# A decoder layer on one core: query products 512 tokens wide, staged three units ahead

## Chip, cores and metric

The kernel runs on one core of a Trainium2 chip. The time is the device time of one execution in microseconds (us), median of the runs shown. Engines: TensorE (PE: matmuls and transposes; PEld is its weight load), VectorE (DVE), ScalarE (ACT), GpSimd (POOL), and SyncE (SP), which here only issues DMAs.

## What is computed

A decoder layer on x of 16 x 64 tokens, width 512, in float32. Cut to what matters:

```python
x = layernorm(x + self_attention(x))        # 32 heads of 16, 8 kv heads, rotary, causal
# second attention: H, KVH, D = 32, 8, 128
q = (x @ Wq).reshape(b, 64, 32, 128); k, v = (ctx @ Wk), (ctx @ Wv)   # 8 kv heads
q = q * cos + rotate_half(q) * sin          # k alike; cos, sin by position
a = softmax(where(mask == 0, -1e9, q @ k.T / sqrt(128)))
x = layernorm(x + (a @ v) @ Wo)
# feed-forward with a selection of rows and columns by clusters
dots = softmax(x @ centroids.T / 0.1); hits = dots > 0.01
y = where(any(hits, 1)[:, None] & any(hits, 0)[assignments][None, :], x @ weight.T + bias, 0)
out = layernorm(x + y)
```

## The kernel before

Everything stays in SBUF, tokens in 8 tiles of 128. Every float32 operand of a large product is split: `copy` on ACT (line 885) rounds it to the array's format ("high"), `low` on DVE (line 1379) or a subtraction on POOL makes the rest ("low"), and a product is three passes, high x high, high x low, low x high (`PASSES`).

The second attention runs as 32 units: a group g (0 to 7) is one kv head with its four query heads, and c (0 to 3) is a pair of token tiles, 256 tokens; unit u = 4 g + c. Each engine has its own program, and a function `slot(u, g, c)` in each writes out by hand what that engine does for the unit; slots 0 to 3 and the last are unrolled, the groups between run in a loop. The engines are held together by semaphores that count.

PE in a slot: `out_proj(u - 1, 1)` (12 matmuls of 512 columns, line 651, the second half of the last unit's output product), the query products of unit u + 2 for the first head pair (`q_pair`, line 424, 24 matmuls of 256), the key and value products of unit u + 1 (`kv_pair`, 24 of 256), `p_turn(u)` (four transposes of the probabilities, line 618), 12 matmuls of the second head pair, `pv(u)` (value products, line 635, 12 of 256), the other 12, `k_turn(u + 1)` (line 644), `out_proj(u, 0)`, and `scores(u + 1)` (lines 665 and 667). In slots 0 to 2 two context tiles are turned first (`ctx_turn`, line 608).

The softmax chain of a unit goes through all engines: `corrections` (ACT), `masked_max2` (DVE, lines 1596 to 1602), `shift` (POOL, line 1290), `exponents` (ACT, line 1049), `total2` (DVE, lines 1606 and 1608), `normalise` (POOL, line 1295), then `p_turn` on PE. Then `p2_high` and `p2_low` round the probabilities for `pv`, and `at2_high` and `at2_low` its result for `out_proj`.

Queries take this way: PE leaves them in banks 0 and 1; DVE multiplies them with the cosine and sine tables (`rope2_q`, lines 1538 and 1539, into `u1q` and `u2q`); POOL adds the halves (`sum_q`, lines 1262 and 1263); SP moves them between partitions with four DMAs (`stage_q`, line 354) into `q_st`; ACT and DVE round them (`q_high`, `q2_low`), with `q_high(u + 1)` ahead of `exponents(u)` in ACT's order from unit 3 on; `scores` uses them. Keys go `rope2_k`, `sum_k` (line 1267), `k_turn`, `k_high`, `k2_low`.

Weights of a group arrive in SBUF once a group: `load_kv` in c = 0, `load_q` (1024 KB into `w2q_raw`) in c = 1, `load_o` in c = 2 into the same place. The query weights of the next group are rounded at the end of the slot with c = 1, two of the four low parts by POOL (`wq_low`, line 1271) and two by DVE; key and value weights in c = 2 (POOL, line 1277), output weights in c = 0 (`wo_low`, POOL line 1282 and DVE).

The tail: units 30 and 31 have no query products any more. The slots of these units are written out apart and hold feed-forward work besides: `fw_turn` (line 764, transposes of its weights), `x3_turn` (line 770, of the normalised tiles), `cluster_dots` (777, 779), `dots_turn` (788), `dense(t)` (795 and 800, twelve matmuls and one for the bias), and after them the counts (869, 872), from which DVE gets the row mask (line 1844) and then does `choose` (1851) and the statistics of each tile.

## Time and profile before

| | us |
|---|---|
| median of 3 runs | 824.31 (824.14 to 825.51) |
| profiled execution | 824.27, span 822.5 |
| PE busy | 765.3 |
| DVE busy | 623.6 |
| POOL busy | 391.8 |
| ACT busy | 319.4 |

The span is the time from the first to the last instruction of the one execution that the profiler took; the rest of its 824.27 us lies around it. Busy time of an engine leaves out waits, branches and the issuing of DMAs. Two things are not in the table and have to be read from the trace: at which places the busiest engine is not busy, and what ended its wait there.

### The profile page before, as it was taken

The numbers are of one execution on the slowest core, as the hardware profiler recorded it, in microseconds if no ns is written. First come the engines' busy times: TensorE is split into PE (matmuls) and PEld (weight loads), VectorE is DVE, ScalarE is ACT, GpSimd is POOL, SyncE is SP. The second block draws the span as 40 slices with busy tenths as digits, with TensorE's granted clock in tenths as the row PEclk, the third lists the DMA queues.
The fourth block names the chain that finished last, engine by engine and source line by source line (L and its number), as shares of the span: only waits on it lengthen the run. The fifth ranks groups of instructions, "written<-read, shape, count | busy, mean of one in ns | idle before, by whom it ended". The sixth has DMA issues, their size and how long they took to land.

```text
span 822.5 us, 15514 instructions
## 1 busy us (share of the span) xinstructions
PE 765.3 (93%) x5520; PEld 691.1 (84%) x5520; DVE 623.6 (76%) x1179; ACT 319.4 (39%) x669; POOL 391.8 (48%) x415
## 2 busy tenths in 40 slices
PE   3689999989899999999999999999999999998894
PEld 2677777779899998999999899999989999997773
DVE  4678888877887777678677767767776777788767
ACT  4455555562443323333332333333232333324313
POOL 7566666664544354444445444544444454443102
PEclk9899999999999999999999999999999999999998
DMA  9500004012333222123322212322221322131002
GB/s 256 124 18 17 16 16 118 3 55 52 85 104 96 52 78 78 27 58 84 87 51 77 77 26 66 84 79 51 77 77 26 75 82 73 45 84 27 1 1 103
DMA packets 104048, 53.50 MB, mean 65 GB/s; under 512 B 80208, under 2 KB 89552, under 8 KB 104016
## 3 DMA queue, kind: packets, MB, share of 16 engines
q1 hardware_dynamic: 103184, 51.51, 24.0%
q10 hardware_dynamic: 576, 1.05, 0.4%
q0 software_dynamic: 256, 0.52, 0.2%
q8 instruction: 19, 0.31, 0.2%
q14 instruction: 13, 0.11, 0.0%
HBM read 32.62 MB, written 2.10 MB: 42 GB/s over the span
## 4 chain that ended last, share of the span: by engine, by line
PE 70%; DVE 15%; issue 8%; POOL 3%; ACT 2%; DMA 1%; SPq 1%; DVEq 0%; ACTq 0%; POOLq 0%
PE bank L424 30%; PE bank L651 18%; PE s_bank L665 4%; DVE arena_r L1379 4%; PE bank L474 2%; PE s_bank L667 2%; PE bank L635 2%; PE bank L498 2%; DVE small L1467 2%; DVE arena_f L1461 1%; PE s_bank L635 1%; POOL arena_f L1295 1%; PE s_bank L498 1%; DMA arena_f<-in_L_attn_Wo 1%; PE bank L618 1%
## 5 line engine op out<-in xcount | busy, mean ns | idle before, releaser
L424 PE MATMUL bank<-arena_r 128*128 128x256 f32 (+1 forms) x2496 | 334.6, 290 | 2.8 <-DVE arena_r L1379 2.0
L424 PEld LDWEIGHTS bank<-arena_r 128*128 128x128 f32 x2496 | 313.3, 191 | 14.3 <-issue 2.4
L885 ACT ACTIVATE arena_r<-bank 128x256 fp32r<-128x256 f32 (+2 forms) x250 | 105.4, 459 | 227.7 <-PE bank L618 98.1
L651 PE MATMUL bank<-arena_r 128*128 128x512 f32 x768 | 191.5, 398 | 0.0
L651 PEld LDWEIGHTS bank<-arena_r 128*128 128x128 f32 x768 | 139.7, 189 | 27.3 <-DVE arena_r L1379 0.6
L1379 DVE TENSOR_TENSOR arena_r<-bank,arena_r 128x256 fp32r<-128x256 f32 (+2 forms) x218 | 100.3, 487 | 57.8 <-ACT arena_r L885 57.6
L885 ACT ACTIVATE arena_r<-arena_f 128x512 fp32r<-128x512 f32 (+2 forms) x178 | 103.8, 637 | 85.6 <-DMA arena_f<-arena_f 71.5
L1379 DVE TENSOR_TENSOR arena_r<-arena_f,arena_r 128x512 fp32r<-128x512 f32 (+1 forms) x114 | 115.9, 1030 | 19.1 <-ACT arena_r L885 19.0
L1262 POOL TENSOR_TENSOR arena_f<-arena_f 128x256 f32<-128x256 f32 x64 | 54.2, 846 | 91.6 <-DVE arena_f L1539 91.5
L1290 POOL TENSOR_TENSOR arena_f<-arena_f,small 128x512 f32<-128x512 f32 x32 | 33.4, 1044 | 109.9 <-DVE small L1602 109.9
L1295 POOL TENSOR_TENSOR arena_f<-arena_f,small 128x512 f32<-128x512 f32 x32 | 44.0, 1375 | 64.7 <-DVE small L1608 64.7
L1565 DVE TENSOR_TENSOR arena_f<-bank,arena_f 128x512 f32<-128x512 f32 x64 | 43.9, 686 | 24.2 <-PE bank L651 24.2
L885 ACT ACTIVATE arena_f<-s_bank 128x512 f32<-128x512 f32 (+1 forms) x35 | 20.5, 586 | 100.2 <-PE s_bank L667 92.6
L667 PE MATMUL s_bank<-arena_r 128*128 128x64 f32 x256 | 57.9, 244 | 0.0
L665 PE MATMUL s_bank<-arena_r 128*128 128x128 f32 x256 | 57.3, 295 | 0.0
L885 ACT ACTIVATE arena_r<-s_bank 128x512 fp32r<-128x512 f32 (+1 forms) x99 | 52.2, 528 | 1.1 <-PE s_bank L498 0.7
L1263 POOL TENSOR_TENSOR arena_f<-arena_f 128x256 f32<-128x256 f32 x64 | 50.1, 783 | 0.0
L667 PEld LDWEIGHTS s_bank<-arena_r 128*128 128x128 f32 x256 | 49.0, 191 | 1.2
L665 PEld LDWEIGHTS s_bank<-arena_r 128*128 128x128 f32 x256 | 49.0, 191 | 1.2
L1216 POOL TENSOR_TENSOR arena_f<-arena_f,small 128x512 f32<-128x512 f32 x32 | 34.3, 1072 | 32.8 <-DVE small L1463 32.8
L1596 DVE TENSOR_TENSOR arena_f<-s_bank,arena_f 128x512 f32<-128x512 f32 x32 | 22.1, 691 | 36.5 <-ACT arena_f L885 36.5
L1379 DVE TENSOR_TENSOR arena_r<-s_bank,arena_r 128x512 fp32r<-128x512 f32 (+1 forms) x83 | 47.8, 576 | 1.1 <-ACT arena_r L885 0.9
(147 smaller groups left out, 1065.2 us busy)
## 6 DMA issues: line engine op xcount, KB each, us to landing
arena_f<-arena_f SPq DMA_DIRECT2D x128, 128.0 KB, 2.5
arena_f<-in_L_xattn_Wq SPq DMA_DIRECT2D x8, 1024.0 KB, 5.5
arena_f<-in_L_xattn_Wo SPq DMA_DIRECT2D x8, 1024.0 KB, 5.5
arena_f<-in_x SPq DMA_DIRECT2D x8, 256.0 KB, 2.9
arena_f<-in_x SPq DMA_DIRECT2D x1, 2048.0 KB, 15.4
arena_f<-in_L_xattn_Wk SPq DMA_DIRECT2D x8, 256.0 KB, 3.0
arena_f<-in_L_xattn_Wv SPq DMA_DIRECT2D x8, 256.0 KB, 3.3
arena_f<-in_ctx SPq DMA_DIRECT2D x8, 256.0 KB, 3.1
```

What stands on the lines that cost most here:

```text
L424: mm = pe.matmul(bank, lhs(a, c), rhs(b, c), start=(c == 0 and n == 0), stop=(c == chunks - 1 and n == 2))
L651: mm = pe.matmul(BO2[i][:], at2[a][:, h, i * P:(i + 1) * P], w2o_s[b][:, h, :], start=(h == 0 and n == 0), stop=(h == HG - 1 and n == 2))
L665: pe.matmul(BS2[h][:, at:at + 2 * S], high, kT2[:, :, b * S:(b + 1) * S], start=True, stop=False, skip_group_check=True)
L667: mm = pe.matmul(BS2[h][:, at + S:at + 2 * S], low_, kT2[:, 0, b * S:(b + 1) * S], start=False, stop=True, skip_group_check=True)
L885: act.activation(dst, src, ACT.Copy).then_inc(done, 1)
L1216: pool.tensor_tensor(cut(p1[u], b=8, k=S), cut(sc1[u % 2], b=8, k=S), bcast(mx1[u], 2, S), ALU.subtract).then_inc(s_sub, 1)
L1262: pool.tensor_tensor(u1q[:, 0, j, :], u1q[:, 0, j, :], u2q[:, 1, j, :], ALU.subtract).then_inc(c_qs, 1)
L1263: pool.tensor_tensor(u1q[:, 1, j, :], u1q[:, 1, j, :], u2q[:, 0, j, :], ALU.add).then_inc(c_qs, 1)
L1290: pool.tensor_tensor(cut(p2, b=8, k=S), cut(sc2, b=8, k=S), bcast(mx2, 2, S), ALU.subtract).then_inc(c_sub, 1)
L1295: pool.tensor_tensor(cut(p2, b=8, k=S), cut(p2, b=8, k=S), bcast(sm2, 2, S), ALU.mult).then_inc(c_pn, 1)
L1379: dve.tensor_tensor(dst, src, f32(high), ALU.subtract).then_inc(done, 1)
L1565: dve.tensor_tensor(y, banks[6 + i][:], y, ALU.add).then_inc(c_acc, 1)
```

## The change

Query products of units 2 to 31 are made 512 tokens wide: one head pair j for the two units of a token half cp, so that a *turn* k (2 to 31) serves two units with one head pair. A turn is run in slot u for k = u + 3 (turns 2 and 3 both in slot 0), and half of its second bank's products stand to either side of `pv`. Units 0 and 1 keep the narrow form. `rope2_q` works bank by bank on 512 columns, `sum_q` is two additions of 512 columns in place of four of 256, at one place of the slot; `stage_q` moves one head pair of two units in four DMAs to `q_high_st` or one of two `q_low_st`. Query weights are loaded and rounded by halves (`load_half`): heads 2 and 3 in c = 1, heads 0 and 1 in c = 3 of the group before, their low parts all on POOL. Late context tiles get buffers of their own. In the tail, the feed-forward weight turns and the first two `x3_turn` stand in unit 29, the 30th, `dense(0)` in unit 30, and the orders of `norm_tile`, `pick`, `x3_turn`, `dense` and of the banks are changed.

```diff
+        def turn_of(g, c):
+            j, ahead = (c + 1) % 2, c + 2 + c % 2
+            return j, (ahead % UN) // 2, g + ahead // UN
+        def staged(u, c):
+            return 128 * u + 128 if isinstance(u, int) and u < 2 else 64 * (u + 1 - c % 2) + 192
 # SyncE
-                sp.wait_ge(c_qs, 4 * u + 4)
+                sp.wait_ge(c_qs, 2 * k + 2)
+                if starts_with(u):
+                    sp.wait_ge(c_wkl, 2)
+                    load_half(1, 0)
+                    stage_q(2, 0, 1)
+                    sp.wait_ge(c_wol, 4)
...
+                elif c == 3 and is_group(g + 2):
+                    sp.wait_ge(c_wkl, 2 * g + 4)
+                    load_half(g + 2, 0)
+                if is_unit(u + 3):
+                    stage_q(u + 3, j, cp)
 # TensorE
+            def q_turn(k, j, cp, f, chunks=range(EC)):
+                if chunks[0] == 0:
+                    pe.wait_ge(c_rq, 2 * k + f - 1)
+                tok = slice(4 * cp * P, 4 * cp * P + 4 * P)
+                for e in chunks:
+                    for n, (a, b) in enumerate(PASSES):
+                        mm = pe.matmul(BQ2[f][:], w2q_s[a][:, e, j, f, :], xT[b][:, e, tok],
+                                       start=(e == 0 and n == 0), stop=(e == EC - 1 and n == 2))
+                if chunks[-1] == EC - 1:
+                    mm.then_inc(c_q, 1)
...
-                if not first:
+                if first:
+                    pe.wait_ge(s_x1l, T)
+                    q_turn(2, 0, 1, 0)
+                    q_turn(2, 0, 1, 1)
+                else:
                     out_proj(u - 1, 1)
-                if q_next:
-                    pe.wait_ge(c_wql, 4 * g2 + 4)
-                    q_pair(u + 2, c2, 0)
+                    if q_next:
+                        pe.wait_ge(c_wql, 4 * gq + 2 * j + 2)
+                        q_turn(u + 3, j, cp, 0)
                 if kv_next:
                     pe.wait_ge(c_wkl, 2 * g1 + 2)
                     kv_pair(u + 1, c1)
                 p_turn(u)
-                if q_next:
-                    pe.wait_ge(c_rq, 2 * u + 4)
-                    q_proj(c2, 1, 0)
+                if first:
+                    q_turn(3, 1, 1, 0)
+                elif q_next:
+                    q_turn(u + 3, j, cp, 1, range(0, 2))
                 pv(u, c, first)
-                if q_next:
-                    q_proj(c2, 1, 1).then_inc(c_q, 1)
+                if first:
+                    q_turn(3, 1, 1, 1)
+                elif q_next:
+                    q_turn(u + 3, j, cp, 1, range(2, 4))
 # GpSimd
+            def sum_q(k):
+                pool.wait_ge(c_rq, 2 * k + 2)
+                pool.tensor_tensor(u1q[:, 0], u1q[:, 0], u2q[:, 1], ALU.subtract).then_inc(c_qs, 1)
+                pool.tensor_tensor(u1q[:, 1], u1q[:, 1], u2q[:, 0], ALU.add).then_inc(c_qs, 1)
...
+                if c == 3 and is_group(g + 2):
+                    wq_low(g + 2, 0)
+                    wq_low(g + 2, 1)
 # VectorE
+            def rope2_q(k, cp, f):
+                dve.wait_ge(c_q, 2 * k + f + 1)
+                if f == 0:
+                    dve.wait_ge(d_qs, 64 * k + 128)
+                tok = slice(4 * cp * P, 4 * cp * P + 4 * P)
+                dve.tensor_tensor(u1q[:, f], banks[f][:], cosT[:, tok], ALU.mult)
+                dve.tensor_tensor(u2q[:, f], banks[f][:], sinT[:, tok], ALU.mult).then_inc(c_rq, 1)
...
-                if split and c == 1:
-                    wq_low(g + 1, 2)
-                    wq_low(g + 1, 3)
...
 # VectorE, unit 31
-            norm_tile(4)
             masked_max2(v, c)
+            norm_tile(4)
             accumulate(v - 1, c - 1, 1)
...
-            dve.tensor_tensor(pair_sum[:], ident[:, 0:NC], ident[:, NC:P], ALU.add).then_inc(f_ps, 1)
```

## Rows read from the trace of the kernel before

**Rows 1.** Page, part 1: busy us, share of the span, instructions

```profile
PE 765.3 (93%) x5520; PEld 691.1 (84%) x5520; DVE 623.6 (76%) x1179; ACT 319.4 (39%) x669; POOL 391.8 (48%) x415
```

**Rows 2.** Busy time by stage: length, then PE, PEld, DVE, ACT, POOL, clock

```profile
243.99:709.25 465.26, 462.19 (x3391) 427.42 (x3390) 341.51 (x625) 158.69 (x350) 216.01 (x223) 1.00 0.25 66
...
726.89:744.53 17.64, 17.64 (x132) 16.40 (x132) 13.51 (x30) 4.82 (x11) 6.99 (x9) 1.00 0.38 101
744.53:763.55 19.02, 16.51 (x120) 14.29 (x120) 16.45 (x37) 9.61 (x21) 3.83 (x5) 1.00 0.12 26
763.55:784.37 20.82, 18.25 (x92) 14.43 (x92) 16.02 (x35) 5.88 (x18) 3.77 (x5) 0.92 0.00 1
```

**Rows 3.** Timeline, a slot with c = 1: start, length, instructions, idle before

```profile
441.01 2.60 PEld L651 LDWEIGHTS bank<-arena_r 128*128 128x128 f32 x12
443.64 5.93 PEld L424 LDWEIGHTS bank<-arena_r 128*128 128x128 f32 x48
449.52 0.25 PEld L618 LDWEIGHTS bank<-ident,arena_f 128*128 128x128 f32 x2
...
454.22 0.69 DVE L1538 TENSOR_TENSOR arena_f<-bank,arena_f 128x512 f32<-128x512 f32 x1
```

**Rows 4.** Who waited for whom, whole span, PE: total, times, longest

```profile
PE bank L618 <- POOL arena_f L1295: 6.5, 8, 2.6
```

**Rows 5.** Timeline, the slot with c = 2 behind it

```profile
458.65 2.60 PEld L651 LDWEIGHTS bank<-arena_r 128*128 128x128 f32 x12
459.30 2.65 SPq L354 DMA_DIRECT2D arena_f<-arena_f  x4
463.80 1.15 ACT L885 ACTIVATE arena_r<-arena_f 128x512 fp32r<-128x512 f32 x2 [4.32 <-DMA arena_f<-arena_f]
467.94 0.20 PEld L618 LDWEIGHTS bank<-ident,arena_f 128*128 128x128 f32 x2 [0.73 <-POOL arena_f L1295]
477.07 2.60 PEld L651 LDWEIGHTS bank<-arena_r 128*128 128x128 f32 x12
```

**Rows 6.** POOL: two groups (busy, mean ns, idle before), two timeline rows

```profile
L1271 POOL TENSOR_TENSOR arena_r<-arena_f,arena_r 128x512 fp32r<-128x512 f32 x16 | 20.6, 1290 | 28.9 <-ACT arena_r L885 28.9
L1234 POOL TENSOR_TENSOR arena_f<-arena_f 128x512 f32<-128x512 f32 x8 | 10.2, 1280 | 1.2 <-DVE arena_f L1399 0.6
448.84 0.74 POOL L1262 TENSOR_TENSOR arena_f<-arena_f 128x256 f32<-128x256 f32 x1 [0.38 <-DVE arena_f L1539]
456.95 1.17 POOL L1262 TENSOR_TENSOR arena_f<-arena_f 128x256 f32<-128x256 f32 x1
```

**Rows 7.** Timeline, a slot with c = 0

```profile
494.72 2.60 PEld L651 LDWEIGHTS bank<-arena_r 128*128 128x128 f32 x12
505.01 0.41 DVE L1379 TENSOR_TENSOR arena_r<-s_bank,arena_r 128x256 fp32r<-128x256 f32 x1
505.29 0.42 PEld L635 LDWEIGHTS bank<-arena_r 64*128 64x128 f32 x6
507.84 0.20 PEld L644 LDWEIGHTS bank<-ident,arena_f 128*128 128x128 f32 x2 [0.15 <-issue]
```

**Rows 8.** Timeline, slot 0, which follows the first attention

```profile
207.45 0.69 DVE L1379 TENSOR_TENSOR arena_r<-bank,arena_r 128x512 fp32r<-128x512 f32 x1 [0.93 <-ACT arena_r L885]
211.70 3.11 PE L424 MATMUL bank<-arena_r 128*128 128x256 f32 x24 [1.17 <-DVE arena_r L1379]
218.22 0.62 PE L635 MATMUL bank<-arena_r 64*128 64x256 f32 x6 [1.42 <-DVE arena_r L1379]
```

**Rows 9.** Timeline, unit 31 and the end

```profile
767.46 0.69 DVE L1596 TENSOR_TENSOR arena_f<-s_bank,arena_f 128x512 f32<-128x512 f32 x1
773.92 0.44 PE L618 MATMUL bank<-ident,arena_f 128*128 128x128 f32 x2 [2.57 <-POOL arena_f L1295]
778.63 5.89 PE L651 MATMUL bank<-arena_r 128*128 128x512 f32 x24
799.97 0.69 DVE L1844 CAST mask_i<-bank 128x512 int32<-128x512 f32 x1 [1.93 <-PE bank L872]
```

More of the change, by code:

```diff
@@ L394, in _ @@
                 load_ctx(t)
-            stage_q(1)
+            stage_first(1)
             for u in range(UN):
                 slot(u, 0, u)
-            with sp.Fori(1, G2 - 1) as g:
+            with sp.Fori(1, G2 - 2) as g:
                 for c in range(UN):
                     slot(UN * g + c, g, c)
+            for c in range(UN):
+                slot(UN * (G2 - 2) + c, G2 - 2, c)
             sp.wait_ge(c_wkl, 2 * G2)
@@ L754, in _ @@
                 slot(u, 0, u)
-            with pe.Fori(1, G2 - 1) as g:
+            with pe.Fori(1, G2 - 2) as g:
                 for c in range(UN):
                     slot(UN * g + c, g, c)
-            for u in range(U - UN, U - 2):
-                slot(u, G2 - 1, u % UN)
+            for c in range(UN):
+                slot(UN * (G2 - 2) + c, G2 - 2, c)
+            slot(U - UN, G2 - 1, 0)
             def fw_turn(c):
@@ L811, in _ @@
             fw_turn(1)
+            p_turn(v)
+            pe.wait_ge(f_wl, 1)
+            fw_turn(2)
+            pv(v, v % UN, False)
+            k_turn(v + 1, False)
+            pe.wait_ge(f_wl, 2)
+            fw_turn(3)
+            pe.wait_ge(f_wl, 3)
+            x3_turn(0)
+            out_proj(v, 0)
+            pe.wait_ge(f_wl, 4)
+            x3_turn(1)
+            scores(v + 1, False)
+            v = U - 2
+            out_proj(v - 1, 1)
+            kv_pair(v + 1, UN - 1)
             pe.wait_ge(d_fc, 16)
@@ L816, in _ @@
             mm.then_inc(f_cT, 1)
+            pe.wait_ge(f_xl, 2)
+            dense(0, range(0, 3))
             p_turn(v)
-            pe.wait_ge(f_wl, 1)
-            fw_turn(2)
-            pe.wait_ge(f_wl, 2)
-            fw_turn(3)
+            dense(0, range(3, EC))
             pe.wait_ge(f_cl, 1)
@@ L1079, in slot @@
                     act.wait_ge(c_q, 2 * u + 6)
-                    for h in range(HG):
-                        wq_high(g + 1, h)
+                    wq_high(g + 1, 2)
+                    wq_high(g + 1, 3)
                 if split and c == 2:
@@ L1115, in _ @@
                 slot(u, 0, u)
-            with act.Fori(1, G2 - 1) as g:
+            with act.Fori(1, G2 - 2) as g:
                 for c in range(UN):
                     slot(UN * g + c, g, c)
-            for u in range(U - UN, U - 2):
-                slot(u, G2 - 1, u % UN)
+            for c in range(UN):
+                slot(UN * (G2 - 2) + c, G2 - 2, c)
+            slot(U - UN, G2 - 1, 0)
             def fw_high(c):
@@ L1354, in root @@
                 pool.tensor_tensor(rstd8[:, t:t + 1], var8[:, t:t + 1], half8[:, 0:1], ALU.pow).then_inc(f_pow, 1)
-            for u in range(U - UN, U - 2):
-                slot(u, G2 - 1, u % UN)
+            slot(U - UN, G2 - 1, 0)
             root(0, 0)
+            shift(U - 3)
             root(1, 1)
+            normalise(U - 3)
+            sum_k(U - 2)
+            root(2, 2)
             shift(U - 2)
-            root(2, 2)
             root(3, 3)
@@ L1723, in _ @@
                 slot(u, 0, u)
-            with dve.Fori(1, G2 - 1) as g:
+            with dve.Fori(1, G2 - 2) as g:
                 for c in range(UN):
                     slot(UN * g + c, g, c)
-            for u in range(U - UN, U - 2):
-                slot(u, G2 - 1, u % UN)
+            for c in range(UN):
+                slot(UN * (G2 - 2) + c, G2 - 2, c)
+            slot(U - UN, G2 - 1, 0)
             def norm_tile(t):
@@ L1763, in pick @@
             def pick(t):
+                dve.wait_ge(f_sel, 1 + sum(t >= b for _, b in GROUPS))
                 dve.wait_ge(f_dense, t + 1)
```

345 lines of the change are left out of this document (210 added, 135 removed).

## The prediction

> **What bounds the kernel now.** I read the busy line first, then busy time and clock by stage, then who waited for whom, then one stretch of the main loop in order of time. TensorE (PE) is the busiest engine, with 93% of the span [rows 1]. Split by stage, the 32 units of cross attention are the body: from 243.99 to 709.25 us PE is busy 462.2 of 465.3 us at its full clock (1.00 granted, 2.4 GHz), and the loose stretches are the last two units, from 744.53 us on [rows 2], and the place where the loop is entered [rows 8]. So in the loop a microsecond of matmul time taken away is a microsecond of span, unless the softmax chain beside it becomes later than PE. I call a *slot* the work from one `out_proj(u - 1, 1)` to the next, c its place among the four of a group. The slot with c = 1 takes 17.64 us (first load of weights at 441.01, the next slot's at 458.65) [rows 3, 5], the one with c = 2 takes 18.42 (458.65 to 477.07) [rows 5], and c = 3 17.65 (to 494.72) [rows 7]. With c = 2 PE waits for `normalise`; the waits list eight such idles, 6.5 us [rows 4], of which unit 31 has 2.57 [rows 9] and unit 30 0.9, so six of about 0.5 in the loop.
>
> **Why c = 2 is late.** The staged queries of the next unit are issued by SyncE (SP) at 459.30, ScalarE can round them at 463.80 (4.50 us later), and its exponentials stand behind them; `normalise` and then `p_turn`, the four transposes, come at 467.94, 4.14 us after the landing and 9.29 into the slot [rows 5]. In c = 1 `p_turn` starts 8.51 us into it (441.01 to 449.52), led by PE's own queue [rows 3].
>
> **1. Wide products.** Before, a unit's queries are 48 matmuls of 256 columns; after, 24 of 512, for 30 turns (units 0 and 1 keep the old form). Starts of weight loads give the spacing: 12 of 512 columns take 2.63 us (441.01 to 443.64), 219 ns each; the 48 of 256 take 5.88 (443.64 to 449.52), 122.5 each [rows 3]. 48 x 122.5 - 24 x 219 = 0.62 us a turn; I take 0.60, since a switch of width costs a little. Bounds: 0.5 to 0.65. In slots 1 to 28 that is 28 x 0.60 = 16.8 us; the turns of units 2 and 3 are both in slot 0.
> The rows put a matmul of 256 columns 13 ns above half of one of 512 (122.5 against 109.5). The Trainium skill, TensorE: Matmul & The Clock Gate, Back-to-back issue gap, gives N/2.4 + 2.5 ns for one matmul after another, so two of 256 would cost only some 3 ns more than one of 512: an estimated 0.08 us a turn, 2 us in all. This trace disagrees with it at 256 columns, and the row decides; what that outcome would be here is rival C.
>
> **2. Staging.** A turn k now serves a head pair of two units, three slots ahead. Its sums on GpSimd (POOL), before four of 256 a unit in two pairs (0.74 us where DVE is away), are two of 512 at the end of the slot; the nearest row is the first attention's sum of two 512-wide arrays, 1280 ns [rows 6]. The four DMAs carry the same 128 KB each. In odd slots (c = 1, 3) the queries of the next unit come from the turn just made, in even slots from one a slot older. So the late landing of c = 2 goes: -6 x 0.78 (18.42 - 17.64) = -4.7 us. The odd slots get a new date. The slot's last ropes start at 454.22, 13.2 into it, led by the end of the query products [rows 3], so at 12.6 after; two of about 0.64 give 13.9, two sums of 1.28 less their overlap 16.4, the issue 16.46; the slot is 17.04 long, so SP issues 0.58 before its end, the queries land 3.92 into the odd slot, and `p_turn` can go at 8.1. PE arrives at 2.63 + 2.63 + 24 x 0.1225 = 8.2. Forecast: no idle, with 0.1 us to spare. If sums run 0.3 us longer each, it is 14 x 0.5 = 7 us.
>
> **3. Slots with c = 0.** VectorE (DVE) there also does one `wo_low` ahead of `p2_low`; the second `p2_low` runs from 505.01 for 0.41 us, 10.7 after the slot's start at 494.72 (the first ends at 10.3), and PE starts the value products at 505.29, 10.57 [rows 7]. After, PE could be there at 9.95 and the DVE date doesn't move (it isn't led by PE): 0.4 idle. 7 x 0.4 = +2.8 us; bounds 0 to 0.6 each. `sum_k` no longer stands behind a query sum, which frees the 0.17 us that the k turns of c = 0 wait (0.15 idle at 507.84) [rows 7]: about -0.8 in all.
>
> **4. Rounding of weights.** DVE loses two `wq_low`, POOL makes all four, two at the end of c = 1 and two of c = 3, each 1290 ns [rows 6]. In c = 1 they end 16.4 + 2.55 = 19.0, 1.95 into c = 2, where PE asks for them at 2.63 after `out_proj`: hidden with 0.7 spare. The shift of the softmax needs POOL at 3.3 into a slot: hidden too. The halves of the weights are loaded nearly a slot ahead of their rounding: nothing.
>
> **5. The front.** Before, slot 0 idles 1.17 us ahead of the key products and 1.42 ahead of the value products [rows 8]. After, it first waits for `x1_low` of the last tile (207.45 + 0.69, against a start at 207.41): +0.8. Then 48 wide matmuls, 10.5 us, in place of 48 narrow, 5.9. They cover the first idle; the value products wait again about 0.6 for DVE, which has two more ropes ahead of `p2_low`. I get the end of slot 0 at 228.05 against 225.46: +2.6. In slot 1 `q_turn(4)` asks for weights of group 1 at 231.5. The chain: rope of turn 3 waits for the staging of turn 2 to land (issue about 220.2, plus 4.5), ropes to 227.6, sums to 230.15, two roundings to 232.7: 1.2 idle, less the 0.6 of its narrow products: +0.6. Bounds for the two together: +1 to +6.
>
> **6. The tail.** Slots 29 to 31 now have no query products; feed-forward turns and one `dense` more stand in them. Slot 29 was 17.64 full of PE work [rows 2]. After: 5.6 us of `out_proj` and keys, 1.0 of `fw_turn`, then `p_turn` at about 8.75 (landing 3.93, plus 4.14, plus statistics and a `norm_tile` on DVE ahead of `total2`); 2.1 idle; then value products 2.2 later, `out_proj(u, 0)` 2.1 behind them (DVE's `at2_low`), scores to 17.95: +0.3. Slot 30 was 19.02; by the same chain it is 18.15, with `dense(0)` inside: -0.9. In slot 31 the mask step no longer waits behind `norm_tile(4)`: it starts about 1.8 in place of 3.9 us into the slot (767.46), `p_turn` comes at 8.7 in place of 10.37 (773.92), `pair_sum` is gone from DVE's part of the chain, and `x3_turn(4)` no longer stands before the value products: the last `out_proj` ends at 18.5 in place of 20.8 (778.63 + 5.89 by its rows, 784.37 by the start of its successor): -2.3 [rows 2, 9]. Behind it runs the chain statistics, `x3_turn(7)`, cluster dots, hits, the two matmuls of counts; 799.97 is the date of the row mask, and from then on DVE is busy without a gap to the end [rows 9]. `pick(1)` costs 0.45 on it; half a `dense` fewer ahead of the second matmul and `pick(3)` out of it give back 1.35: -0.9. Since DVE sets the end, the `dense` moved forward gains nothing there.
>
> **The sum**, against the profiled execution (span 822.5, time 824.27; the median of the runs is 824.31): front +2.6 + 0.6; slots 2 to 28: 27 x 0.60 = -16.2 (the 28th is in the +0.6 of slot 1), -4.7, -0.8, +2.8; tail +0.3 - 0.9 - 2.3 - 0.9. Together -19.5: span 803.0, time 804.8.
>
> **Rivals.** *A, as above*: 801 to 809. *B, staged queries land late in odd slots.* For it: only 0.1 us of slack, and POOL's 256-wide sums already stretch from 0.74 to 1.17 us (456.95) while DVE works on the weights [rows 6]. Against: at that point DVE works on PSUM. Late by 0.5 to 0.8 in 14 slots it costs 7 to 11 us: 812 to 816. *C, no gain by width*: a wide query product takes twice a narrow one. Then 30 x 0.60 = 18 us are lost, of which the idles that PE no longer has in c = 0 give back 2.8: 820, a gain of half a per cent. Against: the output products have the same widths and operands and take 219. *D, slower.* One mechanism: POOL's two sums are stretched throughout as that one is (1.6 times, 4.1 us in place of 2.5). Landing is 1.6 late, 1.5 idle in 14 odd slots (+21), and weights come at 3.6 in place of 1.95 in c = 2, +1 in 7 slots: 805 + 28 = 833. It turns to a loss once the sums take more than about 3.6 us (19.5 gained against 14 + 7 slots). Beside it stands the Trainium skill, GPSIMD Engine Reference, Key points: it shares its SBUF interfaces with VectorE and contends with instructions of two SBUF inputs. The trace agrees with it in the 1.17 us; that DVE reads PSUM where the new sums stand is the reason for the small chance.
>
> **Chances.** A 0.68, B 0.21, C 0.04, D 0.04, and 0.03 for better than A (tail chains shorter than I count). The range 800.5 to 813.5 takes in A and the better half of B. A measurement of this kernel can tell about 0.2%, 1.6 us. Faster 0.92, same 0.03, slower 0.05.
>
> **What would show it.** In the profile after: 512-column matmuls at 219 ns in the query lines; slots of 17.05 with c = 1, 2, 3 and about 17.45 with c = 0; no idle of PE behind `normalise` in c = 2. B shows as ScalarE waiting for the DMA beyond 4.1 us in odd slots and PE behind `normalise`; D as sums of 2 us. I am wrong by the front if slot 1 starts after 230, and by the tail if slot 31 starts less than 15 us earlier than now (763.55).

## The result, and the profile after

The changed kernel takes 817.78 us (median of 4 runs, 817.54 to 818.55) beside 824.47 us for the kernel before in the same comparison: ratio 0.9921 (95% interval 0.9906 to 0.9935). That is a gain of 6.7 us where I had forecast 19.5, so the time lies outside the range of 800.5 to 813.5, on its slow side. The profiled execution has a span of 816.0 us, against 822.5.

The busy line of the page, which answers to [rows 1]: TensorE is still at 93%; it has 720 instructions less, and only 6.7 us less of busy time.

```profile
PE 758.6 (93%) x4800; PEld 649.0 (80%) x4800; DVE 607.5 (74%) x1165; ACT 317.6 (39%) x669; POOL 392.2 (48%) x369
```

Busy time by stage answers to [rows 2] (length, PE, PEld, DVE, ACT, POOL, granted clock, DMA share, GB/s). The stretches are the slots 2 to 28, slot 29, slot 30, slot 31 up to the last output product's end, and the rest.

```profile
247.51:721.42 473.91, 472.12 (x2872) 405.38 (x2871) 340.62 (x638) 163.24 (x365) 223.83 (x190) 1.00 0.27 69
721.42:741.10 19.68, 16.59 (x108) 14.62 (x108) 16.12 (x35) 8.31 (x17) 4.85 (x5) 0.91 0.15 35
741.10:759.84 18.74, 17.14 (x109) 14.07 (x109) 14.42 (x31) 6.62 (x15) 4.86 (x5) 1.00 0.00 1
759.84:778.07 18.23, 16.94 (x91) 13.51 (x91) 15.40 (x33) 5.79 (x18) 3.61 (x4) 1.00 0.00 1
778.07:816.00 37.93, 24.18 (x115) 18.36 (x113) 26.48 (x69) 9.55 (x20) 5.47 (x10) 0.90 0.15 56
```

From the starts of the slots (first load of weights) the 6.5 us of the two profiled spans split as follows:

| part | before | after | difference | forecast |
|---|---|---|---|---|
| start of slot 0 | 206.51 | 205.38 | -1.1 | 0 (no part of the change) |
| slots 0 to 2 | 55.96 | 60.35 | +4.4 | +2.6 |
| slots 3 to 28 | 464.39 | 455.69 | -8.7 | -18.3 |
| slot 29 | 17.65 | 19.68 | +2.0 | +0.3 |
| slot 30 | 19.02 | 18.74 | -0.3 | -0.9 |
| slot 31 to the end | 58.97 | 56.16 | -2.8 | -3.2 |

The -1.1 us ahead of slot 0 are no gain of the change: the other two profiled executions of the changed kernel reach slot 0 some 1.3 and 2.3 us later than this one, with a mean granted clock of 0.87 and 0.79 in their first 40 us for 0.91 here (0.87 before).

Ten of the 13 us that are missing are in the loop. There the slots with c = 1, 2 and 3 take 17.40 to 17.46 us (but for unit 5's, 19.03), where before had 17.64 to 17.67 (18.33 to 18.44 with c = 2), and those with c = 0 17.56 (17.80 to 17.83). So the late landing of c = 2 went as forecast; of what was to come from the width a third did. Of the eight waits for `normalise` [rows 4] three are left, one in the loop and those of slots 29 and 31:

```profile
PE bank L690 <- POOL arena_f L1420: 4.1, 3, 1.8
```

The timeline of TensorE shows where. First a slot of the kernel before that [rows 3] shows by its loads of weights, now by the matmuls themselves (start, length, instructions):

```profile
441.04 2.99 PE L651 MATMUL bank<-arena_r 128*128 128x512 f32 x12
443.87 5.92 PE L424 MATMUL bank<-arena_r 128*128 128x256 f32 x48
449.62 0.38 PE L618 MATMUL bank<-ident,arena_f 128*128 128x128 f32 x2
...
449.98 1.67 PE L424 MATMUL bank<-arena_r 128*128 128x256 f32 x12
451.57 0.62 PE L635 MATMUL bank<-arena_r 64*128 64x256 f32 x6
...
452.48 1.70 PE L424 MATMUL bank<-arena_r 128*128 128x256 f32 x12
454.02 0.38 PE L644 MATMUL bank<-ident,arena_f 128*128 128x128 f32 x2
```

Then the same slot after, and below it the loads of weights of its first three groups:

```profile
459.58 2.99 PE L723 MATMUL bank<-arena_r 128*128 128x512 f32 x12
462.41 2.88 PE L658 MATMUL bank<-arena_r 128*128 128x512 f32 x12
465.13 3.04 PE L484 MATMUL bank<-arena_r 128*128 128x256 f32 x24
468.00 0.38 PE L690 MATMUL bank<-ident,arena_f 128*128 128x128 f32 x2
...
468.35 1.64 PE L658 MATMUL bank<-arena_r 128*128 128x512 f32 x6
469.92 0.62 PE L707 MATMUL bank<-arena_r 64*128 64x256 f32 x6
...
470.82 1.68 PE L658 MATMUL bank<-arena_r 128*128 128x512 f32 x6
472.34 0.38 PE L716 MATMUL bank<-ident,arena_f 128*128 128x128 f32 x2
...
459.55 2.60 PEld L723 LDWEIGHTS bank<-arena_r 128*128 128x128 f32 x12
462.18 2.68 PEld L658 LDWEIGHTS bank<-arena_r 128*128 128x128 f32 x12
464.90 3.05 PEld L484 LDWEIGHTS bank<-arena_r 128*128 128x128 f32 x24
```

The reader is to take starts of matmuls, one group to the next: 12 of 512 columns take 465.13 - 462.41 = 2.72 us, 227 ns each, and 48 of 256 columns 449.62 - 443.87 = 5.75 us, 120 ns each. The unbroken half of a turn thus goes from 24 x 120 = 2.88 to 2.72, 0.16 us. The other half is cut into two short groups, which stand between transposes (`p_turn`, `k_turn`) and the value products with their 64 rows; I call this a change of tile form. These groups hardly move: 449.98 to 451.57 is 1.59 before and 468.35 to 469.92 is 1.57 after; 452.48 to 454.02 is 1.54 and 470.82 to 472.34 is 1.52. Together 0.20 us a slot, and that is what the slots show. The loads tell another story because they run ahead: the first load of a group stands 0.23 us before its matmul (462.18 against 462.41), but at the first group of a slot, which follows short matmuls, only 0.03 (459.55 against 459.58). The 2.63 us from which I took 219 ns began at such a first load and ended at one that was already ahead.

### The profile page after: what moved, and what is told of

It is laid out like the page before. It is cut to its first block, busy times and chain, and to the rows that moved or that the text cites. A ratio compares the mean times of both kernels' runs of the same rounds, so it can differ in the third digit from the quotient of the medians.

```text
span 816.0 us, 13861 instructions
## 1 busy us (share of the span) xinstructions
PE 758.6 (93%) x4800; PEld 649.0 (80%) x4800; DVE 607.5 (74%) x1165; ACT 317.6 (39%) x669; POOL 392.2 (48%) x369
## 4 chain that ended last, share of the span: by engine, by line
PE 64%; DVE 19%; issue 6%; POOL 4%; ACT 2%; DMA 2%; SPq 2%; DVEq 0%; ACTq 0%; POOLq 0%
PE bank L723 17%; PE bank L658 17%; PE bank L484 10%; DVE arena_r L1512 5%; PE s_bank L737 3%; PE bank L534 2%; PE s_bank L739 2%; PE bank L707 2%; PE bank L558 2%; DVE small L1600 2%; DVE arena_f L1594 1%; PE s_bank L707 1%; ACT arena_r L979 1%; PE s_bank L558 1%; DMA arena_f<-in_L_attn_Wo 1%
## 5 line engine op out<-in xcount | busy, mean ns | idle before, releaser
L723 PE MATMUL bank<-arena_r 128*128 128x512 f32 x768 | 192.2, 399 | 0.9 <-DVE arena_r L1512 0.9
L658 PE MATMUL bank<-arena_r 128*128 128x512 f32 x720 | 185.2, 400 | 2.2 <-POOL arena_r L1396 1.6
L723 PEld LDWEIGHTS bank<-arena_r 128*128 128x128 f32 x768 | 139.9, 189 | 28.2 <-DVE arena_r L1512 1.3
L658 PEld LDWEIGHTS bank<-arena_r 128*128 128x128 f32 x720 | 130.7, 188 | 31.5 <-POOL arena_r L1396 2.1
L484 PE MATMUL bank<-arena_r 128*128 128x256 f32 (+1 forms) x1056 | 146.7, 295 | 1.5 <-DVE arena_r L1512 0.6
L484 PEld LDWEIGHTS bank<-arena_r 128*128 128x128 f32 x1056 | 137.4, 191 | 9.0 <-DVE arena_r L1512 1.5
L1512 DVE TENSOR_TENSOR arena_r<-arena_f,arena_r 128x512 fp32r<-128x512 f32 (+1 forms) x100 | 92.9, 937 | 17.6 <-ACT arena_r L979 17.5
L1387 POOL TENSOR_TENSOR arena_f<-arena_f 128x512 f32<-128x512 f32 x30 | 39.2, 1306 | 114.2 <-DVE arena_f L1681 114.2
L1420 POOL TENSOR_TENSOR arena_f<-arena_f,small 128x512 f32<-128x512 f32 x32 | 44.0, 1376 | 61.0 <-DVE small L1750 61.0
L1415 POOL TENSOR_TENSOR arena_f<-arena_f,small 128x512 f32<-128x512 f32 x32 | 34.1, 1065 | 64.9 <-DVE small L1744 64.9
```

Of the source, the lines that this page charges most:

```text
L484: mm = pe.matmul(bank, lhs(a, c), rhs(b, c), start=(c == 0 and n == 0), stop=(c == chunks - 1 and n == 2))
L658: mm = pe.matmul(BQ2[f][:], w2q_s[a][:, e, j, f, :], xT[b][:, e, tok], start=(e == 0 and n == 0), stop=(e == EC - 1 and n == 2))
L723: mm = pe.matmul(BO2[i][:], at2[a][:, h, i * P:(i + 1) * P], w2o_s[b][:, h, :], start=(h == 0 and n == 0), stop=(h == HG - 1 and n == 2))
L1387: pool.tensor_tensor(u1q[:, 0], u1q[:, 0], u2q[:, 1], ALU.subtract).then_inc(c_qs, 1)
L1415: pool.tensor_tensor(cut(p2, b=8, k=S), cut(sc2, b=8, k=S), bcast(mx2, 2, S), ALU.subtract).then_inc(c_sub, 1)
L1420: pool.tensor_tensor(cut(p2, b=8, k=S), cut(p2, b=8, k=S), bcast(sm2, 2, S), ALU.mult).then_inc(c_pn, 1)
```

## The experiments

**The width, undone.** `q_turn` with each product in two runs of 256 columns; all the rest is the changed kernel.

```diff
-                for e in chunks:
-                    for n, (a, b) in enumerate(PASSES):
-                        mm = pe.matmul(BQ2[f][:], w2q_s[a][:, e, j, f, :], xT[b][:, e, tok],
-                                       start=(e == 0 and n == 0), stop=(e == EC - 1 and n == 2))
+                for i in range(chunks[0] * P // width, (chunks[-1] + 1) * P // width):
+                    for e in range(EC):
+                        for n, (a, b) in enumerate(PASSES):
+                            mm = pe.matmul(BQ2[f][:, width * i:width * i + width], w2q_s[a][:, e, j, f, :],
+                                           xT[b][:, e, at + width * i:at + width * i + width],
+                                           start=(e == 0 and n == 0), stop=(e == EC - 1 and n == 2))
```

> The changed kernel with each query product over 512 tokens issued as two of 256 columns, the first half of the columns through all its 12 matmuls and then the second; staging, sums, ropes, POOL's order and the tail stay as changed. So the width is undone and all else is kept. Theory A (the width is worth what the starts of the matmuls give: 0.227 us for 512 columns and 0.120 for 256, 12 x (2 x 0.120 - 0.227) = 0.16 us in each of the two halves of a turn that runs unbroken, and about 0.02 us in each of the halves that end in a change of tile form): the ordinary slot goes from 17.44 to 17.64 us, 28 slots and the four turns of slot 0 add 6 us, about 824 us, as the kernel before. Theory B (my prediction: 0.60 us a slot, from the starts of the weight loads 0.219 and 0.1225): the slot goes to 18.05 us, +17, about 835 us. Theory C (the wait for the value products' low halves on VectorE sets the slot, so the width is idle): no change, 817 to 818 us.

Measured: 822.69 us, beside 817.90 for the changed kernel; its ordinary slots are 17.64 to 17.66 us. Theory A holds by the slots and my price of 0.60 us a slot falls. The medians differ by 4.8 us and not by 6, in part because the slots with c = 0 also take 17.64: the 0.13 us by which they were longer is hidden again. In the timeline both groups of 24 take 2.88 us:

```profile
465.13 3.04 PE L665 MATMUL bank<-arena_r 128*128 128x256 f32 x24
468.01 3.05 PE L484 MATMUL bank<-arena_r 128*128 128x256 f32 x24
470.89 0.38 PE L698 MATMUL bank<-ident,arena_f 128*128 128x128 f32 x2
```

**The repetition** that stood beside it:

> The changed kernel once more, beside the next three, so that each difference is taken on one chip. Expected: the ratio to the kernel before stays 0.992 (817.8 us beside 824.4). In the trace of its first execution the slots stood 17.43 to 17.46 us apart where before has 17.64 to 17.66, save one, unit 5's, with 19.03 us, in which TensorE waited 1.57 us for the normalised weights. Theory A (an accident of the transfers in the window of that execution): the 19.03 us slot is gone or elsewhere, and the others are 17.43 to 17.46 again. Theory B (the order of the queue in the loop's first pass): it comes back in the same slot with 18.9 to 19.1 us.

Measured: 817.90 us, ratio 0.9913 (0.989 to 0.9937). The ordinary slots are 17.40 to 17.46 again (slot 27 takes 17.69, behind a late landing), and unit 5's slot is the long one again: theory B by its place, though 19.40 us lies above its 18.9 to 19.1. More on it below.

**Only the cut half narrow.** The same edit for the second dimension half alone (`width = 2 * P if f == 1`).

> The changed kernel with only the second dimension half's product (the one cut in two parts, around the value products) issued in 256 columns; the first, unbroken one keeps 512. Theory A (at a change of tile form TensorE waits for the last matmul's end, 0.39 us after its start for 512 columns and 0.28 for 256, which takes back most of what six wide ones gain): +0.02 to 0.05 us in each of its two places, slots at 17.48 to 17.54 us, +1 to +3 us in all, 819 to 821 us. Theory B (the gain is by the columns, wherever they run): 2 x 0.08 us, slots at 17.60 us, +4.5 us, 822.3 us.

Measured: 818.61 us; slots of 17.50, +0.06. The two places take 1.60 and 1.55 us in place of 1.57 and 1.52. Theory A by the slots; the 0.7 us of the medians is within their spread. Six wide matmuls gain 0.03 us here where six in a long stream gain 0.08. (Unit 5's slot takes 17.50 here.)

```profile
468.38 1.67 PE L665 MATMUL bank<-arena_r 128*128 128x256 f32 x12
469.98 0.62 PE L715 MATMUL bank<-arena_r 64*128 64x256 f32 x6
...
470.88 1.70 PE L665 MATMUL bank<-arena_r 128*128 128x256 f32 x12
472.43 0.38 PE L724 MATMUL bank<-ident,arena_f 128*128 128x128 f32 x2
```

The mechanism of theory A, a wait at the end of the group, is not what the trace shows. Read one by one, the starts in the first of the two places lie 314, 231, 236, 228, 233 and 327 ns apart in the changed kernel, and 201, then ten of 116 to 121, then 209 in this one. The long interval ahead of the value products costs both widths nearly the same (100 and 89 ns more than in a stream), and so does the one behind the transposes (87 and 81). In the second place the last interval, ahead of transposes, is 232 and 123: no such wait at all. Most of the lost gain lies between: the wide ones stand 228 to 240 ns apart all through these short groups, the narrow ones 113 to 125. The first group of a slot, 12 wide ones behind short matmuls and with no change of form after them, starts alike (316, 237, 228, 232, 232) and only then reaches 227.

**Four runs of 128 columns**, the same edit with `width = P`:

> The changed kernel with each query product over 512 tokens issued as four of 128 columns, one after the other. It looks for the form of the cost of a matmul. Theory A (columns at 2.4 GHz and a fixed 13.5 ns with each matmul, as 0.227 us for 512 and 0.120 for 256 columns give): matmuls start 0.067 us apart, the unbroken half takes 48 x 0.067 = 3.2 us for 2.72, the two cut ones some 0.2 us more each, an ordinary slot 18.3 to 18.4 us, about 25 us more, 843 us. Theory B (no matmul can follow sooner than its weights' load, which at 0.12 us a pair is what set the pace at 256 columns): they stay 0.12 us apart, the slot grows by about 5 us to 22 to 23 us, over 950 us.

Measured: 973.64 us, ratio 1.182; slots of 22.57. My theory A of this run, a fixed cost with each matmul, is wrong, and B holds: 48 matmuls of 128 columns take 479.87 - 474.57 = 5.30 us, 110 ns each, 8% less than the 120 ns of 256 columns.

```profile
474.57 5.47 PE L665 MATMUL bank<-arena_r 128*128 128x128 f32 x48
479.87 3.09 PE L484 MATMUL bank<-arena_r 128*128 128x256 f32 x24
...
474.34 5.55 PEld L665 LDWEIGHTS bank<-arena_r 128*128 128x128 f32 x48
```

**One order in the kernel before.** POOL's part of `slot`, nothing else:

```diff
-                if split and c == 1:
-                    wq_low(g + 1, 0)
                 if is_unit(u + 2):
                     sum_q(u + 2, 1)
                 if split and c == 1:
+                    wq_low(g + 1, 0)
                     wq_low(g + 1, 1)
```

> The kernel before with one edit: in the second slot of four POOL does both sums of the second head pair ahead of both query weight lows, no longer between them. Nothing of the change's width, staging or tail. Theory A (the late landing behind POOL's 2.6 us per low is all that the third slot's 18.4 us are made of): the third slots go from 18.34 to 18.44 to 17.65 us, 6 or 7 times 0.75 = 4.7 us less, about 819.7 us, ratio 0.994. Theory B (TensorE waits for something else there, or the second low comes too late for the products that need it): less than 1.5 us of it is gained, over 822.5 us.

Measured: 819.32 us, ratio 0.993 (0.9913 to 0.9946); slots with c = 2 are 17.64. That is 5.2 of the 6.6 us that the changed kernel gains in the same comparison (4.5 us by the six slots of the profile, 0.75 each): the landing date alone is worth most of it, and one moved order has it without any wide product.

**Two orders in the kernel before**: the same and, on VectorE, both `p2_low` ahead of `rope2_k`.

> The kernel before with two orders changed and nothing else: in the second slot of four POOL does the sums ahead of the query weight lows (as in before_order), and VectorE makes the low halves of the transposed weights ahead of the key ropes in every slot (as in p2_first). Theory A (TensorE's own stream sets all slots once the two waits are gone): every slot 17.64 to 17.66 us, so 0.2 us less than before_order in each of seven first slots, 1.4 us, about 818.0 us: as fast as the changed kernel within a measurement, without one wide product. Theory B (the first slot of four waits for something else): 17.80 to 17.86 us stay there, 819.3 us as before_order.

Measured: 818.20 us; the slots with c = 0 stay at 17.81 to 17.84. Theory B: there TensorE waited for the key turns behind POOL's sums (start of L644 1.64 us behind the query products where 1.54 is usual), hardly for the value products (the same slots take 17.80 to 17.86 in before_order). The second order gained nothing in this kernel. The 1.1 us between the two medians are not in the slots. This kernel, which has no wide query product, can't be told from the changed one in the same comparison (after_third below: 817.99).

```profile
503.47 1.70 PE L424 MATMUL bank<-arena_r 128*128 128x256 f32 x12
505.11 0.43 PE L644 MATMUL bank<-ident,arena_f 128*128 128x128 f32 x2
```

**The same order on VectorE in the changed kernel:**

```diff
-                if kv_next:
-                    rope2_k(u + 1, c1, False)
                 p2_low(u, 0)
                 p2_low(u, 1)
+                if kv_next:
+                    rope2_k(u + 1, c1, False)
```

> The changed kernel with VectorE making the low halves of the transposed weights (p2_low) ahead of the key ropes and no longer behind them, in every slot. Theory A (0.16 us of the 0.21 us beyond six matmul intervals ahead of the value products is the wait for the last matmul's end, which no engine's order mends): the ordinary slot goes from 17.44 by 0.05 at most, to 17.39, the first slot of four from 17.56 to 17.40, 0.05 x 21 + 0.15 x 7 = about 2 us less. Theory B (all of it is the wait for VectorE): 0.2 us in the ordinary slot, 17.24, and 0.3 in the first of four, about 6 us less. Theory C (the later ropes make the key sums late for the key turns): the slots get longer than 17.44.

Measured: 816.60 us. Slots with c = 0 go from 17.56 to 17.43, the others stay at 17.43, and the six wide matmuls ahead of the value products still take 1.57 us. So in the ordinary slot TensorE doesn't wait there for VectorE's rounding; in c = 0 0.13 us was VectorE's. Of the theories A comes nearest, without its 0.05 us in the ordinary slot.

**The front.** In slot 1 of the changed kernel TensorE stands before the wide products; POOL has the weight lows behind the sums:

```profile
232.77 3.02 PE L658 MATMUL bank<-arena_r 128*128 128x512 f32 x12 [1.64 <-POOL arena_r L1396]
...
227.24 1.28 POOL L1387 TENSOR_TENSOR arena_f<-arena_f 128x512 f32<-128x512 f32 x1 [6.07 <-DVE arena_f L1681]
...
229.73 2.99 POOL L1396 TENSOR_TENSOR arena_r<-arena_f,arena_r 128x512 fp32r<-128x512 f32 x2
```

```diff
-                if is_unit(u + 3):
-                    sum_q(u + 3)
                 if starts_with(u):
                     wq_low(1, 0)
                     wq_low(1, 1)
+                if is_unit(u + 3):
+                    sum_q(u + 3)
```

> The changed kernel with one edit in the first slot: POOL makes the two lows of the next query weights (ready 224.1 us into the execution by ScalarE's copies) ahead of the sums of unit 3's queries (which wait for VectorE's ropes until 227.2) and no longer behind them. Theory A (TensorE's 1.6 us at 231 us wait for these lows alone): it goes, the second slot takes 18.4 to 18.8 us for 20.2, about 1.6 us less in all, 816.2 us. Theory B (behind the lows POOL's shift of the scores or a later landing is as late): under 0.5 us is gained.

Measured: 816.51 us, ratio 0.9916 (0.99 to 0.9933). The interval can't tell it from the changed kernel, but the trace shows the mechanism: the lows run at 224.43, the sums still begin at 227.03, and the wait is gone: slot 1 takes 18.36 us in place of 20.24.

```profile
224.43 2.54 POOL L1396 TENSOR_TENSOR arena_r<-arena_f,arena_r 128x512 fp32r<-128x512 f32 x2 [3.47 <-ACT arena_r L979]
227.03 1.27 POOL L1387 TENSOR_TENSOR arena_f<-arena_f 128x512 f32<-128x512 f32 x1
```

**Slot 29 and the clock.** Here TensorE waits three times and then runs at half clock (1.2 GHz granted). Waits, and then the stretch (length, PE, granted clock, DMA share, GB/s), of the changed kernel:

```profile
729.96 0.44 PE L690 MATMUL bank<-ident,arena_f 128*128 128x128 f32 x2 [1.77 <-POOL arena_f L1420]
731.57 0.66 PE L844 MATMUL bank<-ident,arena_f 128*128 128x128 f32 x4 [0.95 <-DVE arena_r L1512]
732.59 0.69 PE L707 MATMUL bank<-arena_r 64*128 64x256 f32 x6 [0.36 <-DVE arena_r L1512]
...
733.42:735.42 2.00, 2.00 (x14) 0.50 0.03 8
```

Nine matmuls that nobody reads fill the waits (`filler(n)` is n times `pe.matmul(banks[4][:], w2kv_s[0][:, 0, 0:P], xT[0][:, 0, 0:4 * P])`):

```diff
+            filler(6)
             p_turn(v)
+            filler(3)
             pe.wait_ge(f_wl, 1)
```

> The changed kernel with nine matmuls of 512 columns whose result nobody reads put into TensorE's idle stretches of the 30th slot: six between the first feed-forward weight turns and the turn of the attention weights, three ahead of the third feed-forward turn. It computes the same. Theory A (the granted clock falls to 0.5 from 732 to 736 us because TensorE stood still for 2.7 of the 4 us before): it stays at 1.00, the slot takes 18.0 to 18.6 us for 19.68, about 1.3 us less in all. Theory B (the clock falls for the transposes or for another reason): it falls as before and the slot stays at 19.6 us or grows by what the nine matmuls overrun, 0.3 us.

Measured: 818.46 us, ratio 0.9938 (0.9921 to 0.9954), no gain. In its profile the clock is 1.00 throughout and slot 29 takes 18.09 us. But two kernels without them, with the same three waits, also have 1.00: p2_first (18.10) and loop_later (18.09). The other nine profiled executions of the changed kernel and its variants without the fillers have the fall, the two with them (order_clock below is the second) don't. The fall of the clock thus explains 1.6 us of the profiled slot 29; that the standing still brings it about is likely and not shown, and neither is that it costs the median anything.

**All orders together**: front_order, p2_first, and in slot 30 the bias rounded behind `p2_low` with its product behind `k_turn`; then the same with the fillers; and the changed kernel beside them.

> The changed kernel with front_order's edit, p2_first's edit and one in the 31st slot: VectorE rounds the bias behind the transposed weights' low halves and no longer ahead of them, and TensorE adds the bias product behind the key turns. If the parts add up: front 1.6 us, first slots of four 0.13 x 6 = 0.8 us, the wait of 1.0 us at 752 us in the 31st slot gone (0.5 to 1.0 us, as the wait ahead of the output product behind it may grow): about 3.2 us less than the changed kernel's 817.8, 814.6 us. If the bias wait is only passed on to the output product: 815.3 us. If they don't add (the p2 order already took what the front order takes): over 816.2 us.

> order_all with keep_clock's nine idle matmuls in the 30th slot. In keep_clock's profile the clock stayed at 1.00 and that slot took 18.09 us for 19.65, but its median of six, 818.5 us, was no lower than the changed kernel's 817.9. Theory A (the clock falls there in most executions, and keeping it up is worth 1.5 us): about 813.2 us. Theory B (it falls in few executions, as p2_first's profile with 18.10 us and no fall shows, so the nine matmuls gain nothing in the median): the same as order_all within 0.5 us.

> The changed kernel beside the other three, for the differences on one chip: 817.8 us, ratio 0.992. In its profile the 30th slot takes 19.65 us if the clock falls there and 18.1 us if it doesn't; unit 5's slot 19.0 to 19.4 us if its late landing belongs to the first pass of the loop, 17.43 if it was chance twice.

Measured: 814.62 us, ratio 0.9893 (0.9866 to 0.992); 813.71, ratio 0.9888 (0.9871 to 0.9906); 817.99, ratio 0.9933 (0.9909 to 0.9957). For order_all that is the 814.6 us forecast if the parts add up, and they do so in the trace: slot 30 takes 17.55 for 18.74, the front and c = 0 as in the single runs. Both medians are below both kernels'; the interval of order_clock lies wholly below that of the changed kernel in this comparison, that of order_all overlaps it. Between the two new ones 0.9 us is within their spread (812.0 to 819.1 in all), so the fillers stay unproven.

**Unit 5's slot.** In nine of the ten profiled executions of the changed kernel and its variants with the loop in its place (width128 left out) the slot of unit 5 takes 18.3 to 21.2 us; the 21.2, in order_all, holds a fall of the granted clock besides (0.59 on average from 309 to 313 us, behind a wait of 2.0 us). The rows: SP's issue, ScalarE's rounding and TensorE's wait there, then the issue and rounding in an ordinary odd slot.

```profile
300.23 2.66 SPq L399 DMA_DIRECT2D arena_f<-arena_f  x4
306.55 1.16 ACT L979 ACTIVATE arena_r<-arena_f 128x512 fp32r<-128x512 f32 x2 [4.98 <-DMA arena_f<-arena_f]
310.73 0.44 PE L690 MATMUL bank<-ident,arena_f 128*128 128x128 f32 x2 [1.37 <-POOL arena_f L1420]
...
476.47 2.65 SPq L399 DMA_DIRECT2D arena_f<-arena_f  x4
480.94 1.15 ACT L979 ACTIVATE arena_r<-arena_f 128x512 fp32r<-128x512 f32 x2 [3.13 <-DMA arena_f<-arena_f]
```

It is 6.3 us from issue to rounding for 4.5. Three of the four transfers land on time, 2.5, 3.1 and 3.9 us behind the first issue (2.4, 3.1 and 3.8 in the ordinary slot); the last lands at 6.3 for 4.5. Two kernels move the code and nothing else, by writing out group 1 ahead of the loop (`Fori(2, G2 - 2)`), and by writing out all groups.

> The changed kernel with the second group (units 4 to 7) written out ahead of the loop on every engine, so that the loop begins with unit 8. The work and its order are the same. Theory A (the landing of the staged queries, 6.3 us after their issue in unit 5's slot for 4.5 elsewhere, is late in the first pass through the loop's code): slot 5 takes 17.45 and the slot of unit 9, the same place in the new first pass, 19.0 to 19.4 us; the total stays at 818. Theory B (it belongs to unit 5, by its place behind the front): slot 5 keeps 19.0 to 19.4 and slot 9 17.45. Theory C (code run for the first time is late wherever it stands): both slots take 19 us, or slot 7 and others, and the total grows by 1.5 to 4 us.

> The changed kernel with no loop over the groups: units 4 to 27 are written out on every engine, in the same order. Theory A (entry of the loop): no slot of 19 us is left, about 1.6 us less than the changed kernel, 816.2 us. Theory B (unit 5 itself): one slot of 19.0 to 19.4 us, at unit 5, 817.8. Theory C (code run for the first time): the odd slots in which a block of code is fetched while the four transfers are under way take 18.5 to 19.4 us, up to twelve of them, 825 to 835 us.

Measured: 817.71 and 819.58 us. loop_later has unit 5's slot at 17.41 and one of 18.31 at unit 11 (landing 5.7 us behind the issue); no_loop has 19.18 at unit 11 and 19.30 at unit 25 (6.5 and 6.7 us). B falls; A and C missed the place, since neither named unit 11. What the late ones have in common is in the list of DMA queues for the 4.6 us behind each issue. Over twelve executions with 168 such landings in odd slots, 15 have a line q8 there, of kind "instruction", which I read as the fetching of code (packets, MB, share), and these 15 took 5.0 to 7.0 us; the others took 4.5, but for one of 4.9, whose q8 packet started 0.03 us ahead of the issue. Packets of 8 KB on queue q14, of the same kind, stand in seven more of the stretches, that of 4.9 us among them; the other six took 4.5. Here the changed kernel from 300.23 and no_loop from 649.92:

```profile
q8 instruction: 1, 0.02, 1.3%
...
q8 instruction: 1, 0.02, 1.7%
```

The packet meets the transfers in two ways. Where it starts about 1 us behind the first issue (loop_later's 11th unit, 1.12), SP issues the fourth transfer late, 2.95 us behind the first for 2.0; where it starts 3.4 to 4.3 us behind, all four are issued on time and the last lands 1.8 to 2.5 us late. It is not a rule without exceptions: the kernel before and both its variants have a q8 packet 4.2 us behind the issue of slot 30's queries, and these land at 4.5 us; and in even slots, where nothing waits for it, no_loop has two landings at 5.7 us with only an 8 KB packet beside them.

## Why the prediction was wrong, step by step

**What bounds the kernel: right.** TensorE sets the slot before and after; a slot follows the sum of its matmul spacings.

**Step 1, width: right in direction, three times too large, and the main error.** The term "27 x 0.60 = -16.2" came to 27 x 0.21 = -5.7 us. Two mistakes are in it. The spacing was read from starts of weight loads, which made 512 columns 8 ns too cheap and 256 columns 2.5 ns too dear: 12 x (2 x 120 - 227) = 0.16 us for a half, where the loads gave 12 x (2 x 122.5 - 219) = 0.31. And I let all of a turn gain alike, while its second half is cut into two groups of six, each of which gains 0.02 to 0.03 us and not 0.08. The trace of before had it: the output products of 512 columns, by matmul starts, take 443.87 - 441.04 = 2.83 us for 12, not 2.63, and the one group of 12 that stands behind others of 512, the first `dense`, takes 770.94 - 768.21 = 2.73, 227.5 ns each:

```profile
768.21 2.89 PE L795 MATMUL bank<-arena_r 128*128 128x512 f32 x12
770.94 0.40 PE L800 MATMUL bank<-arena_r,share 128*128 128x512 f32 x1
```

The result lies closer to the 820 us of rival C, to which I gave 0.04, though not by its rule. The Trainium skill (TensorE: Matmul & The Clock Gate, Back-to-back issue gap) gives N/2.4 + 2.5 ns, 216 and 109 ns; the runs show 227 and 120. (By it the gain would be 24 x 2.5 ns = 0.06 us a turn, not the 0.08 that I wrote.) The same section says that in a stream the spacing is set by load and matmul together, and calls the formula that of a single matmul; the 110 ns at 128 columns agree with that in kind, and I had weighed only the formula. Its own figures for such a stream, 81 ns at 128 columns and 131 at 512, lie below the 110 and 227 measured here.

**Step 2, staging: right.** The c = 2 slots gave 4.5 us for 4.7 (before_order has them alone), and in odd slots SP issues 0.54 us before the slot's end (476.47; forecast 0.58) and the rounding starts 3.9 into the next (forecast 3.92), with sums of 1.29 us. Rivals B and D did not come about. The slack was larger than the 0.1 us forecast, since TensorE reaches `p_turn` 8.4 us into the slot. One landing, unit 5's, came late, beside a code fetch that I had not thought of: -1.6 us of the gain in the profile.

**Step 3, c = 0: direction right, size too large.** VectorE's wait was 0.13 us, not 0.40: TensorE comes later than I reckoned, by what step 1 did not gain. The k turns' 0.17 us went, as before_orders shows from the other side.

**Step 4, rounding of weights: right in the loop.** No wait for them in any slot with c = 2.

**Step 5, the front: +4.4 in place of +2.6 us.** Slot 0 came near the forecast (+2.9 for +2.6), but by two errors that cancel: its 48 wide products took 11.4 us and not 10.5, and the wait of 0.6 us ahead of the value products did not come. Slot 1 took +1.7 for +0.6: the chain to its wait was right (lows done at 232.7, as measured), but the wait was 1.64 us for 1.2 and cost 1.9 (front_order's slot 1 is shorter by that), and its products gave back 0.2 us for 0.6. Front_order shows that the wait hung on one order on POOL.

**Step 6, the tail: slot 31 right, the end by luck, slot 29 wrong (+2.0 for +0.3).** From slot 31 on it is -2.8 us for -3.2: `p_turn` comes 8.8 us into the slot (forecast 8.7), the last output product ends at 18.2 (forecast 18.5), and the date of the row mask goes from 799.97 to 794.58 [rows 9]:

```profile
768.65 0.44 PE L690 MATMUL bank<-ident,arena_f 128*128 128x128 f32 x2 [0.96 <-POOL arena_f L1420]
...
794.58 0.69 DVE L2010 CAST mask_i<-bank 128x512 int32<-128x512 f32 x1 [1.01 <-PE bank L967]
```

Behind the last output product I had forecast -0.9 us from a shorter chain to the row mask. That chain got longer, 16.5 us (778.07 to 794.58) for 15.6, and what stands behind the mask 1.1 us shorter, for which I had nothing; 0.6 us of this may be the one execution, since before_order, the same code there, is as much shorter from slot 31 to the end (58.35 for 58.92).

In slot 29 the waits were forecast (2.1 us ahead of `p_turn`; measured 1.77, and 0.95 and 0.36 behind it), the half clock after them was not: 1.6 us. In slot 30 the bias rounding ahead of `p2_low` cost 1.0 us that I had costed at nothing; order_all has it back.

Sum of the misses against the 13.0 us: width in slots 3 to 28 10.1, front 1.8, slot 29 1.7, unit 5 1.6, slots 30 and 31 1.0, less 2.0 for c = 0 and the 1.1 by which slot 0 began early: 13.1.

## What to carry to other kernels

Read the pace of a stream of matmuls from the starts of the matmuls, over a group between two groups of the same kind, and never from the weight loads, which run ahead by a varying amount. Price a change of width separately for each place: a group of six behind a change of tile form gained a third, or less, of what six in a long stream gain. Before building on a wide rearrangement, look for the one wait that it also removes: here two lines on POOL had three quarters of the gain.

## What the runs showed of the hardware

- Products of fp32r operands, a load of weights to each matmul, at 2.4 GHz: 110 ns apart at 128 columns, 120 at 256, 227 at 512. Halving 256 columns saves 10 ns; from 256 to 512 it is 107 ns for 256 columns, 0.42 ns each, which is one column in a cycle of 2.4 GHz.
- Between two changes of tile form (128 rows, 64 rows, transposes) six matmuls of 512 columns took 1.52 to 1.57 us where six intervals are 1.36; twelve of 256 took 1.54 to 1.60 where twelve are 1.44. Some 0.1 us of it is the first interval, behind the change, and 0.1 the last where 64-row products follow; ahead of transposes the last interval is the usual one.
- Four transfers within SBUF of 128 KB are rounded 4.5 us after their issue, within 0.05; with a code fetch of 0.02 MB in the same stretch 5.0 to 7.0 us in 15 of 15 odd slots of the twelve executions, but 4.5 in slot 30 of the kernel before and its two variants. The Trainium skill (Runtime: NRT & Kernel Launch, Terms) says that instruction memory is refilled in blocks of 16 KiB, which fits the one packet seen. That the fetch delays the landing is what the coincidence suggests; how it does so is open.
- The granted clock fell to 1.2 GHz for about 3.4 us (6.8 in narrow) after TensorE had stood still for 3.1 of 4.4 us in slot 29, and did not fall in two others with the same waits (p2_first, loop_later).
- Executions of one kernel spread by 6 to 7 us (813.9 to 821.2 for the changed kernel), while its slots with c = 1, 2 and 3 take 17.40 to 17.46 us in all three traces, but for those with a late landing (units 5 and 27): an edit worth less than a microsecond has to be read from the slots. In every kernel the longer executions are by and large those with the lower mean granted clock (half_narrow: 815.6 us at 0.990, 822.7 at 0.979), so the clock is in this spread; where it fell in the executions without a trace is not known.
